# A graph kernel's edge loop, with the finishing stages one step later and the edge columns in a ring of seven

## What is computed

```python
def _cgconv(x, src, dst, edge_attr, Wf, bf, Ws, bs, gamma, beta, rmean, rvar):
    z = jnp.concatenate([x[dst], x[src], edge_attr], axis=-1)
    msg = jax.nn.sigmoid(z @ Wf + bf) * jax.nn.softplus(z @ Ws + bs)
    summed = jax.ops.segment_sum(msg, dst, num_segments=n)
    cnt = jax.ops.segment_sum(jnp.ones((dst.shape[0],), x.dtype), dst, num_segments=n)
    out = summed / jnp.maximum(cnt, 1.0)[:, None]
    out = (out - rmean) * jax.lax.rsqrt(rvar + BN_EPS) * gamma + beta
    return out + x
x1 = _cgconv(x, ...)
x = _layernorm(x + _cgconv(x1, ...), axis=-1)
```

## Time and profile before

| | us |
|---|---|
| median of 3 timed runs | 2143.16 (2141.11 to 2143.25) |
| span of the profiled execution | 2795.4 |
| busy in it: PE, DVE, ACT, POOL | 1618.1, 1685.4, 1379.6, 1541.2 |

### The profile page before, as it was taken

One profiled execution on the slowest core, in us unless ns is written; L12 is line 12 of the kernel. 1 busy time (PEld: TensorE's weight loads), 2 busy tenths in 40 slices (PEclk: granted clock), 3 DMA queues, 4 the chain that ended last, 5 costly groups with the idle time before them and its releaser, 6 DMA issues. The chain is left out here.

```text
span 2795.4 us, 33286 instructions
## 1 busy us (share of the span) xinstructions
PE 1618.1 (58%) x7507; PEld 1390.7 (50%) x7507; DVE 1685.4 (60%) x3576; ACT 1379.6 (49%) x2083; POOL 1541.2 (55%) x1590
## 2 busy tenths in 40 slices
PE   6565665566666666666726555555555454454554
PEld 5454555556555565555625444454444444454443
DVE  3566666656656665667536665665656555665567
ACT  3445455545545554555325454554544454454455
POOL 5455565665556665564145555555555555555550
PEclk9777777777677777678867777777777777777776
DMA  8454454454445544454644444444444444454442
GB/s 314 124 148 136 135 147 143 138 151 137 138 143 145 151 145 144 138 155 129 224 152 138 133 138 138 135 144 127 144 138 131 134 138 137 131 144 135 133 136 62
DMA packets 232010, 401.73 MB, mean 144 GB/s; under 512 B 71586, under 2 KB 154906, under 8 KB 231863
## 3 DMA queue, kind: packets, MB, share of 16 engines
q0 software_dynamic: 75392, 205.80, 25.3%
q1 hardware_dynamic: 154982, 192.84, 23.2%
q10 hardware_dynamic: 1490, 1.72, 0.2%
HBM read 370.54 MB, written 29.64 MB: 143 GB/s over the span
## 5 line engine op out<-in xcount | busy, mean ns | idle before, releaser
L333 POOL DMA_INDIRECT pre<-s_rows,ends x1568 | 1520.5, 970 | 1125.4 <-DVE soft_ps L584 557.2
L378 PE MATMUL pre_ps<-rhs,lhs 128*128 128x256 f32 x3136 | 1102.5, 513 | 1108.1 <-DVE lhs L564 581.1
L378 PEld LDWEIGHTS pre_ps<-rhs,lhs 128*128 128x128 f32 x3136 | 766.6, 256 | 1275.7 <-issue 685.3
L438 ACT ACTIVATE pre<-pre 128x512 f32<-128x512 f32 x392 | 247.5, 631 | 1323.7 <-DVE pre L580 1064.5
L600 DVE TENSOR_TENSOR sums<-sums,sum_ps 128x128 f32 (+1 forms) x784 | 196.4, 251 | 907.8 <-remote 765.2
L388 PEld LDWEIGHTS sum_ps<-hot,msg 128*128 128x128 f32 x3136 | 526.5, 230 | 49.9 <-DVE msg L591 7.3
L388 PE MATMUL sum_ps<-hot,msg 128*128 128x64 f32 x3136 | 489.2, 304 | 7.0 <-DVE msg L591 6.8
L580 DVE TENSOR_TENSOR pre<-pre_ps,pre 128x1024 f32<-128x1024 f32 x392 | 477.6, 1218 | 23.9 <-PE pre_ps L378 22.6
L443 ACT ACTIVATE logs<-pre 128x1024 f32<-128x1024 f32 x392 | 414.7, 1058 | 12.3
L564 DVE TENSOR_SCALAR lhs<-lhs,base_f,part 64x256 f32<-64x256 int32 x784 | 322.2, 454 | 48.1 <-issue 35.6
L591 DVE TENSOR_TENSOR msg<-soft_ps,logs 128x512 f32<-128x512 f32 x392 | 271.1, 692 | 13.3
(11 more groups left out here) (64 smaller groups left out, 201.6 us busy)
## 6 DMA issues: line engine op xcount, KB each, us to landing
lhs<-dge_and_destination_cols SPq DMA_DIRECT2D x196, 512.0 KB
rhs<-d_rows SPq DMA_DIRECT2D x784, 64.0 KB
pre<-s_rows,ends POOLq DMA_INDIRECT x1568
s_rows<-pre SPq DMA_DIRECT2D x24, 512.0 KB, 5.6
d_rows<-logs SPq DMA_DIRECT2D x12, 512.0 KB
d_rows<-msg SPq DMA_DIRECT2D x8, 512.0 KB
out<-y_out SPq DMA_DIRECT2D x12, 256.0 KB, 2.3
d_rows<-hot SPq DMA_DIRECT2D x4, 512.0 KB
```

The lines of the kernel that those rows point to most:

```text
L333: nc.gpsimd.indirect_dma_start(pre[:, slot(k, j), i, 0:F2], None, s_dram, bass.IndirectOffsetOnAxis(ap=ends[:, k, j * TILES + i, 0:1], axis=0)
L378: ins = nc.tensor.matmul(pre_ps[:, j % 2, i, :], lhs[:, j // 2, edges], rhs[:, j, i // 2, :], start=True, stop=True)
L438: nc.scalar.activation(pre[:, at, :, F2:3 * F], pre[:, at, :, F:F2], ACT.Abs).then_inc(s_abs[j], 1)
```

## The change

Both directions between PE and DVE get one more step. On DVE `sums` handles the step two back (was one), `softplus` and `message` three back (was two), `one_hot` three back (was the step itself), and `add_up` five back (was four). On PE `window_sum` handles four back (was three). The two `add_up` stand together at the end of a DVE step, where before each stood beside `sums`. Registers for `add_up` are loaded twice a group, at j = 0 and j = 1, after `sums`. The buffer `lhs` is a ring of seven single steps, loaded three steps ahead (`AHEAD`) in single transfers of 256 KB; SP waits each step for the product four back, where it waited every second step for the one three back.

```diff
-        lhs = sb("lhs", [P, SLOTS // 2, 2 * STEP], F32)
+        lhs = sb("lhs", [P, RING, STEP], F32)
...
+        def edges_loaded(b, k, j):
+            return (b * SLOTS + ((SLOTS * k + j) // RING + 1)) * 16
...
-            def load_edges(j, edge):
-                sp.dma_start(lhs[:, j // 2, :], d["edge_cols"][:, bass.ds(edge, 2 * STEP)]).then_inc(edge_in[j // 2], 16)
+            def load_edges(at, edge):
+                sp.dma_start(lhs[:, at, :], d["edge_cols"][:, bass.ds(edge, STEP)]).then_inc(edge_in[at], 16)
...
-                for j in range(0, SLOTS, 2):
-                    done(sp, s_prod, g, j, 3)
+                for j in range(SLOTS):
+                    done(sp, s_prod, g, j, SLOTS)
                     sp.sem_inc(passed, 1)
-                    if not (isinstance(g, int) and g == 0):
-                        load_edges(j, blk * GROUP + j * STEP)
                     load_rows(j, bases)
-                    load_rows(j + 1, bases)
+                    if j + AHEAD < SLOTS:
+                        load_edges(slot(k, j + AHEAD), blk * GROUP + (j + AHEAD) * STEP)
+                    else:
+                        load_edges(slot(k, j + AHEAD), blk_next * GROUP + (j + AHEAD - SLOTS) * STEP)
...
                     product(b, k, j)
-                    if at := back(b, k, j, 3):
+                    if at := back(b, k, j, SLOTS):
                         window_sum(at[0], at[2])
...
-                one_back, two_back, four_back = (
-                    back(b, k, j, lag) if live(lag) else None for lag in (1, 2, 4))
+                two_back, three_back, five_back = (
+                    back(b, k, j, lag) if live(lag) else None for lag in (2, 3, 5))
                 if live(0):
                     hot_transposed(b, k, j)
-                if four_back:
-                    done(v, s_added, four_back[0], four_back[2], 1)
-                    add_up(four_back[0], four_back[2], 0, sum_at)
-                if one_back:
-
-                    turn = (b if j == 0 and k == 0 else b + 1)
-                    sums(one_back[0], turn, one_back[1], one_back[2])
-                if four_back:
-                    add_up(four_back[0], four_back[2], 1, sum_at)
                 if two_back:
-                    softplus(two_back[0], two_back[2], slot(two_back[1], two_back[2]))
-                if two_back:
-                    message(two_back[0], two_back[2])
-                if live(0):
-                    one_hot(g, k, j)
+
+                    sums(two_back[0], b if SLOTS * k + j < 2 else b + 1, two_back[1], two_back[2])
+                if five_back and j < 2:
+                    steps = range(SLOTS - 1, SLOTS) if j == 0 else range(SLOTS - 1)
+                    for i, at in enumerate(load_bases(five_back[1], steps)):
+                        sum_at[PAIRS * steps.start + i] = at
+                if three_back:
+                    softplus(three_back[0], three_back[2], slot(three_back[1], three_back[2]))
+                    message(three_back[0], three_back[2])
+                    one_hot(three_back[0], three_back[1], three_back[2])
+                if five_back:
+                    done(v, s_added, five_back[0], five_back[2], 1)
+                    add_up(five_back[0], five_back[2], 0)
+                    add_up(five_back[0], five_back[2], 1)
```

More of the change, by code:

```diff
@@ L101, in graph_layer @@
         ends_in, base_in = each("ends_in", BODY), each("base_in", BODY)
-        edge_in, d_in = each("edge_in", SLOTS // 2), each("d_in")
+        edge_in, d_in = each("edge_in", RING), each("d_in")
         src_in = [each(f"src_in_{k}_") for k in range(BODY)]
@@ L246, in _ @@
                 store_rows(sp, s_dram, s_stage, c, s_out)
-            for j in range(0, SLOTS, 2):
+            for j in range(AHEAD):
                 load_edges(j, j * STEP)
@@ L282, in _ @@
             sp.wait_ge(sp_tab_in, groups * 16 + 16)
+            for j in range(AHEAD):
+                sp.wait_ge(edge_in[j], bodies * (SLOTS * 16) + 16)
             sp.sem_inc(passed, 1)
@@ L376, in product @@
                 for i in range(TILES):
-                    edges = slice(j % 2 * STEP + i * P, j % 2 * STEP + (i + 1) * P)
-                    ins = nc.tensor.matmul(pre_ps[:, j % 2, i, :], lhs[:, j // 2, edges], rhs[:, j, i // 2, :],
-                                           start=True, stop=True)
+                    ins = nc.tensor.matmul(pre_ps[:, j % 2, i, :], lhs[:, slot(k, j), i * P:(i + 1) * P],
+                                           rhs[:, j, i // 2, :], start=True, stop=True)
                 ins.then_inc(s_prod[j], 1)
@@ L404, in _ @@
             groups = bodies * BODY
-            for j in range(1, SLOTS):
+            for j in range(SLOTS):
                 window_sum(groups + (-1), j)
@@ L598, in add_up @@
                 rows = 2 if first else 1
-                into = t["sums"][:, 0:rows, bass.ds(at[PAIRS * j + q], WIN)]
+                into = t["sums"][:, 0:rows, bass.ds(sum_at[PAIRS * j + q], WIN)]
                 ins = nc.vector.tensor_tensor(into, into, sum_ps[:, j % 2, q, 0:rows, 0:WIN], ALU.add)
@@ L603, in _, with load_bases @@
             added_one = sem("added_one")
-            def load_bases(k):
+            def load_bases(k, steps):
                 return nc.values_load_multi_w_load_instructions(
-                    base_i[0:1, k, :], engines=[ENG.DVE], min_val=0, max_val=NPAD - WIN,
+                    base_i[0:1, k, PAIRS * steps.start:PAIRS * steps.stop], engines=[ENG.DVE], min_val=0, max_val=NPAD - WIN,
                     skip_runtime_bounds_check_because="every entry of the table is clamped")[1]
-            def stages(b, k, j, sum_at, live=lambda lag: True):
+            sum_at = {}
@@ L649, in one @@
                             prepare(b, 0, 1 if isinstance(b, int) else b + 2)
-                    stages(b, k, j, sum_at)
+                    stages(b, k, j)
             turns(v, bodies, one)
             groups = bodies * BODY
-            sum_at = load_bases(BODY - 1)
-            for j in range(SLOTS):
-                stages(bodies, 0, j, sum_at, lambda lag, j=j: j < lag)
+            for n in range(5):
+                stages(bodies, n // SLOTS, n % SLOTS, lambda lag, n=n: n < lag)
             for j in range(SLOTS):
```

19 lines of the change are left out of this document (9 added, 10 removed).

## The result

The changed kernel takes **2147.96 us** (median of 11 runs, 2145.58 to 2149.42), the kernel before on the same chip 2142.92 us (11 runs, 2141.11 to 2144.54). The ratio is 1.0023, 95% interval 1.0016 to 1.0031: 5.0 us, or 0.2%, slower. The forecast was 2144, within 2139 to 2148 if its likeliest case held; the result lies just under that upper end.

The account below looks back on a forecast made before the run. It took GpSimd's gathers, issued one behind the other, to set the loop's pace and hide the other costs. All parts were priced at 0 except +0.8 at the layer ends: 2143.2 + 0.8 = 2144 us, range 2075 to 2165.

Parts of the forecast that it names:

- likeliest case: Whole kernel: gathers set the pace and hide the change's costs; 2144 us, by itself 2139 to 2148, chance 0.55.
- The recorded span: Whole kernel: the first recording's 2795.4 us holds 652 us that timed runs lack, so its stalls are not costs yet.
- at least 307 of 765 us not there: VectorE's "remote" waits ahead of node additions: at least 307 of 765 us absent from timed runs, more likely nearly all.
- The gathers set the pace: GpSimd in the loop: gathers start 1.253 us apart, 5.01 us a step of four, and bound the timed runs.
- the first rival: TensorE to VectorE: late counts also hold timed runs, so the change is faster, most likely 2085 to 2130 us; chance 0.29.
- The start stalls: GpSimd waiting for the first softplus once the ring is full: 15.97 us in layer 1, 23.1 in layer 2, perhaps shorter timed.
- sum of 2152.8: GpSimd, whole run: 1964.7 us of gathers plus 188.0 around them, 0.5% above the timed median.
- The ring, SyncE, registers: Gather ring, SP's extra edge transfers and VectorE's registers loaded twice a group: each priced at 0.
- The pair of additions: VectorE: two additions together take 0.61 us, +0.21 a step, 82 us in all, hidden under the gathers.
- the second rival: VectorE bounds the loop, so the paired additions cost their full price: 2225 us; chance 0.07.
- One more step of slack: Between TensorE and VectorE: 4.25 us or more of slack for window-sum waits, priced at 0 in timed runs.
- Ends of a layer: Last step of each layer: `one_hot` stands between message and window sum, 0.42 us, twice: +0.8 us.

Follow-up runs that it names:

- experiment 1: The kernel before, unchanged, recorded again: timed at 2139.38 us, against 2141.17 us for the kernel before in that job.
- experiment 5: The kernel before with only the ring of seven edge buffers and SyncE's new transfers, old order kept: 2140.61 us, ratio 1.0.
- experiments 2 and 3: Three gathers a step instead of four, `sums` taking `w_node` instead of gathered rows: kernel before 1932.23 us (0.9034), changed kernel 1946.28 us (0.9089).
- exp. 4: The changed kernel with the rows of each layer's whole first group loaded ahead of its edges: 2147.5 us, ratio 1.0032.
- exp. 6: The kernel before with only the new order of TensorE and VectorE, keeping the two double edge buffers: 2146.73 us, ratio 1.0026.
- experiment 12: The changed kernel with the window sum's one-hot made one step earlier, two back instead of three: 2149.03 us, ratio 1.0027.
- experiment 7: The kernel before with the transposed one-hots made by a `tensor_tensor` comparison instead of a `tensor_scalar`: 2157.7 us, ratio 1.0075.
- 10: The kernel before with the transposed one-hots made for only 8 of every 256 columns (output not the graph layer's): 2141.32 us, ratio 0.9989.
- experiment 11: The kernel before with ScalarE's second logarithm left in SBUF, from where softplus takes it: 2177.22 us, ratio 1.0158.
- 8: The changed kernel with the transposed one-hots made by a `tensor_tensor` comparison instead of a `tensor_scalar`: 2151.94 us, ratio 1.0048.
- experiment 9: The changed kernel with the window sum's one-hot made for the step just begun, as in the kernel before: 3153.1 us, ratio 1.471.

## Why the prediction was right, and what was missed

**The recorded span proved nothing.** Right, and shown by experiment 1: recorded again, the same kernel took 2137.6 us. The bound of "at least 307 of 765 us not there" was safe; in fact 85 us of waits for window sums are there.

**The gathers set the pace.** Right, shown from three sides: `sums` waits for gathered rows in both new traces, a quarter of the gathers gone takes some 200 us off, and 107 us less work on VectorE takes off 0.1%. In experiment 1 the median spacing is 1.251 us and the mean 1.261. 1568 of these are 1977.6; with 42.0 us before the first gather, 59.2 between the layers and 54.5 after the last (188.0 in the earlier trace rows), and 4.7 more at the filling of the ring, the sum is 2138.0 for a span of 2137.6. The 0.5 to 2.2% that the first rival lived on are gone: they were the disturbed execution's too. The start stalls of 15.97 and 23.1 us are spacings of 2.75 and 4.48 us here, the shorter ones that the prediction left open. That its sum of 2152.8 came so near is in part luck: the 188.0 around the gathers were 32 us too many, while its 1.253 a gather and starts without a stall were 13 and 5 us too few.

**The ring, SyncE, registers.** Priced at 0, shown at 0 for ring and SyncE together (experiment 5). No run has the registers by themselves.

**The pair of additions.** Its 0.61 us was low by 0.12, since it takes 0.73 to the next start. The step as a whole went from 4.25 to 4.33, not to 4.46, because its neighbours became cheaper. The full price with the cover taken away was put at 82 us. VectorE's bare step says 392 x 0.08 = 31, and between experiments 2 and 3 it measured 14, net of what the extra step gave back. By these figures the second rival would have given some 2157 to 2174, not 2225.

**One more step of slack.** Priced at 0 in the timed runs, right: of 85.3 us of waits for window sums 82 go. In experiments 2 and 3 it is visible as well: VectorE's bare step rose by 0.08 us, its mean by only 0.03 to 0.04. I read the rest as slack used; no run had the one without the other.

**Ends of a layer: the term that was mis-sized.** "Twice: +0.8" counted one one-hot and left out that additions come a step later too. The end of layer 1 on VectorE, in the kernel before (experiment 1) and in the changed one:

```profile
1036.43 1.23 DVE L580 TENSOR_TENSOR pre<-pre_ps,pre 128x1024 f32<-128x1024 f32 x1 [2.89 <-DMA pre<-s_rows,ends]
...
1041.32 0.69 DVE L591 TENSOR_TENSOR msg<-soft_ps,logs 128x512 f32<-128x512 f32 x1
1041.93 0.70 DVE L600 TENSOR_TENSOR sums<-sums,sum_ps 128x128 f32 x2
1044.51 0.71 DVE L600 TENSOR_TENSOR sums<-sums,sum_ps 128x128 f32 x2 [1.88 <-PE sum_ps L393]
```

```profile
1038.94 1.22 DVE L586 TENSOR_TENSOR pre<-pre_ps,pre 128x1024 f32<-128x1024 f32 x1 [2.90 <-DMA pre<-s_rows,ends]
...
1044.43 0.41 DVE L578 TENSOR_TENSOR hot<-lane,rel 128x256 f32<-128x256 f32 x1
1044.77 1.54 DVE L606 TENSOR_TENSOR sums<-sums,sum_ps 128x128 f32 x4
1048.02 0.70 DVE L606 TENSOR_TENSOR sums<-sums,sum_ps 128x128 f32 x2 [1.72 <-PE sum_ps L399]
```

Two steps' additions (1.54 us) now stand behind the last message instead of one (0.70), and the last of all waits behind them. From the last `sums` to the end of the last addition it takes 9.79 us instead of 8.79.

The whole difference, from the starts and ends in five traces, in us:

| | last `sums` to last addition, layers 1 and 2 | last addition to next gather | first to last gather, layers 1 and 2 |
|---|---|---|---|
| before (exp. 1) | 8.79, 8.38 | 47.07 | 990.2, 989.8 |
| ring alone (exp. 5) | 8.79, 8.38 | 48.41 | 989.2, 990.2 |
| after | 9.79, 9.25 | 48.84 | 992.7, 990.9 |
| rows first (exp. 4) | 9.79, 9.26 | 47.93 | 991.5, 991.4 |
| order alone (exp. 6) | 9.79, 9.26 | 48.57 | 991.1, 992.6 |

The means of the last three rows less those of the first two give 1.9 for the ways out of the layers, 0.7 between the layers, and 3.7 for the gathers: 6.3 of 6.5 us by which the spans differ (2144.6 against 2138.1). The 1.9 are explained: one third is the one-hot, shown by experiment 12, and two thirds are the later additions, read from the two timelines above. The 0.7 is within what one kernel varies there.

The 3.7 are beyond it (1979.4 and 1980.0 against 1982.9 to 1983.7), and the same traces say where they lie. 1.1 is the first filling of the ring: its two long spacings add up to 7.2 us in both kernels of the old order, to 7.5 to 9.3 in the three of the new. This part may be chance: in experiments 7, 10 and 11 (old order) they are 6.9 to 8.5, in 8 and 12 (new order) 7.0 and 7.4. The other 2.6 are long gathers. Lengthening as in the table above is 16.2 and 15.6 us in the old order and 17.8 to 18.9 in the new, with 151 and 153 long gathers against 164 to 182. More of them start under `hot` (76 to 86, for 67 and 53), about as many under the transposed one-hots (81 to 91, for 79 and 94). That more gathers are long is so in each of the three traces of the new order; why they fall together with `hot` more often there stays open.

So the forecast was 4 us low by two terms: the ways out of the layers, put at 0.8 and measured at 1.9, and the gathers, put at 0, which take 2.6 us more, or 3.7 with the filling of the ring. That the result is still inside the likeliest case's 2139 to 2148, by 0.04 us, is luck; the mechanism, gathers that set the pace and hide the rest, is what the runs show. "Same" was the likeliest, and the interval of the ratio lies on both sides of the 0.2% that was called no change, so the runs do not settle whether to call it the same or slower by a little.

No version here that computes the whole output beats the kernel before: the ring alone equals it.

## What to carry to other kernels

Set a recorded span against the timed runs before any stall in it is believed; where they differ, record again or reason from what the timed runs leave room for. More slack between two engines gains nothing while a third sets the pace, and it is paid for at each end of the loop, where what was hidden is drained in the open. When a lag grows, count each buffer that a wait goes round: one step too few turned overlap into taking turns, for 47%. Where gathers from GpSimd set the pace, look for VectorE instructions with all their inputs in SBUF: here they lengthen the gathers of the kernel before by 16 us in all, and moving one input of softplus from PSUM to SBUF cost 33 more.

## What the runs showed of the hardware

- Gathers issued one behind the other start 1.251 us apart, of which 0.95 is the instruction and 0.30 stands between, by the median of nine of the thirteen new traces (1.254 in experiments 11 and 12). With three gathers a step it is 1.397 (experiments 2 and 3): there the first gather of a step has waited for softplus, starts inside `hot` in 376 of 392 steps, and takes 1.09 us; with the 0.30 behind it that is 1.397.
- The clock that TensorE was granted averages 0.841 in experiment 1 and 0.826 after, and 0.686 in experiment 9, where TensorE stands idle 2.6 to 2.8 us ahead of most products; the one shown takes 3.75 us, nearer to the 3.78 of the earlier trace rows than to the 1.97.
- A VectorE instruction whose inputs all lie in SBUF delays a gather that starts inside it, to its own end: the gather then ends 0.81 to 0.84 us after that end, in 150 of the 151 long ones of experiment 1. Of the 1319 gathers there that start under no such instruction, or less than 0.15 us before its end, one takes over 0.975 us. `sums`, `message`, the additions and, outside experiment 11, softplus have an input in PSUM and delay none. An instruction that starts behind the gather, or just ahead of it (under some 0.04 us for `hot`), doesn't delay it either. The longest gather takes 1.20 us in experiment 1, and 1.46 in experiment 11, under the 0.69 us of softplus, not a whole instruction more, since a gather starts somewhere inside it.
- The Trainium skill, page SBUF — State Buffer, section SBUF: two separate sides, says that VectorE and GpSimd share a pair of ports, which a VectorE operation in a two-port mode, or with two inputs from SBUF against a GpSimd operation that reads SBUF, holds to its end while the other waits. These traces agree: `hot`, the `tensor_tensor` of experiment 7 and softplus in experiment 11 have two SBUF inputs, the gather reads its indices (`ends`) from SBUF, the delay lasts to VectorE's end, and the one that starts first isn't held. The `tensor_scalar` has one tensor input and delays gathers too; whether it runs in a two-port mode, no trace here shows.
